# The order of 64 attention jobs: from unit by unit to a wave of four units, three batches apart

## The chip, the cores and the metric

The kernel runs on one core of one Trainium2 chip. The metric is the device time of one execution in microseconds (us), the median of several runs; lower is better.

## What is computed

Sixteen batches of 256 tokens of width 256 go through four attention units and then through a routed expert layer. Cut to what matters here:

```python
x = x + tanh(g_xattn[0]) * _L0_xattn_ref(ctx_2048, _layernorm(x), L0_xattn_b, itok)   # unit 0: keys and values are the two halves of ctx
x = x + tanh(g_ffn[0])   * _L0_ffn_ref(_layernorm(x), ...)                            # unit 1: self attention + top-2 of 8 dense experts (256 to 256)
x = x + tanh(g_xattn[1]) * _L1_xattn_ref(_layernorm(x), ctx_2048, ...)                # unit 2: self attention over own keys and ctx keys, projection
x = x + tanh(g_ffn[1])   * _L1_ffn_ref(_layernorm(x), ...)                            # unit 3: causal attention, projection, then the routed experts
```

All four attentions have 16 heads of 16 columns. Unit u of a batch needs unit u-1 of the same batch and nothing of another batch.

## The kernel before

`attention_phase` does 64 jobs `(u, b)`, four units by 16 batches, and `expert_phase` does the rest of unit 3 (routing, experts, combination); only the first is touched by the change. A job is a chain of steps. `LOADX` brings x; `LNS`, `LNP`, `LNX` normalise it on VectorE and GpSimd; `XT` turns it on TensorE. `K`, `Q`, `V` project (two turns each on TensorE, read from one of two banks `pre_ps` by ScalarE); in unit 0 `KT` and `XT` stand for K and Q, and `VC` copies the values out of the loaded context on GpSimd. `KSPLIT` and `QSPLIT` split keys and queries into three bf16 parts on GpSimd; `STACKK`, `STACKQ` store these parts to HBM and `ROWSK`, `ROWSQ`, `ROWSC` bring them back stacked by rows (`ks`, `qs`), all issued by SyncE. `S` computes the scores of a head (TensorE into `s_ps`, two banks) and VectorE takes their maximum; `M` and `MT` put the maxima of eight heads into `qs`. `T` computes the scores again, turned (TensorE into `t_ps`, two banks), and ScalarE takes their exponential; `PV` multiplies with the values, `OT` turns and divides. Unit 1 has `GATE`, `GEXP`, six `TOP` steps, `CT`, `MBIAS` and eight `EXPERT` steps; units 2 and 3 have `OTT` and `PROJ`; `FIN` adds to x and `STOREX` stores it. Unit 2 has two sources of keys, so 32 `S` and 32 `T` for 16 heads.

What sets the order: `orders()` plays the steps once, ahead of the build, with the costs in `STAGES`, takes each engine's next step by the soonest start (and by the lower job where two are close), lets no job begin that is `AHEAD_JOBS = 6` or more ahead of the first unfinished one, and writes one fixed list for each engine (`ORDER`). On the chip each engine goes through its own list in that order and waits on semaphores. Which buffer of a ring a job has follows from its place in the list `JOBS`:

```python
JOBS = [(u, b) for u in range(UNITS) for b in range(B)]
NX, NCTX, NPART, NQ, NKV, NO = 5, 2, 2, 3, 4, 3
```

So all 16 jobs of unit 0 come first, then all of unit 1, and so on. Values of the context: unit 0 lays them out in `va` and stores them (`STOREV`, 512 KB a batch, to `vc_d`); unit 2 loads them back (`LOADV`). Rows 96 to 98 of `ks` hold a bias in unit 0 alone; `UNBIAS` clears them on VectorE when the first four jobs of unit 1 take these buffers.

Of the kernel before, what the change touches and what calls it, by code (L numbers as in the profile page):

```python
# [28 lines left out]
G = 2  # L29
# [17 lines left out]

UNITS = 4
JOBS = [(u, b) for u in range(UNITS) for b in range(B)]
# [10 lines left out]

def kv_at(u, b, src=0):

    return (b, B + b, 2 * B + 2 * b + src, 4 * B + b)[u]
# [4 lines left out]
    "LOADX": [("sp", 0.4), ("wire", 4.0)], "LOADC": [("sp", 0.5), ("wire", 9.0)], "LOADV": [("sp", 0.5), ("wire", 6.5)],  # L68
    "VC": [("pool", 0.65)], "STOREV": [("sp", 0.5), ("wire", 8.5)],
# [6 lines left out]
    "UNBIAS": [("dve", 1.8)], "BPROJ": [("pool", 1.27)],  # L76
# [36 lines left out]
def job_steps(u, b):  # L113
# [15 lines left out]
    def kv_before(src):  # L129

        at = kv_at(u, b, src) - NKV
        return next(((v, c, s) for v, c in JOBS for s in range(sources(v)) if kv_at(v, c, s) == at), None)

# [27 lines left out]
    turned = add("XT", 0, s, *free)  # L161
    if u == 0:
        k = add("KT", 0, c, past("STACKK", NPART))
        q = turned
        needs[turned].append(past("STACKQ", NPART)) if past("STACKQ", NPART) else None
    else:
        k = add("K", 0, turned, past("STACKK", NPART))
        q = add("Q", 0, turned, past("STACKQ", NPART))
        values.append(add("V", 0, turned, *values_free(srcs - 1), ("STOREV", 0, kv_at(u, b) - NKV, 0) if u == 1 and b < NKV else None))
    k = add("STACKK", 0, add("KSPLIT", 0, k))  # L170
# [7 lines left out]
    clear = add("UNBIAS", 0, *keys_free(0, 0), *keys_free(0, 1)) if u == 1 and b < NKV else None  # L178
    if u == 1:
        chain = add("GEXP", 0, add("GATE", 0, turned))  # L180
        for n in range(TOPS):
            chain = add("TOP", n, chain)
        chain = add("MBIAS", 0, add("CT", 0, chain))
        experts = [add("EXPERT", (t, e), chain) for t in range(NT) for e in range(0, E, 2)]
    outs = []
    for g in range(G):
        ss = [add("S", (h, src), *rows, *keys[g]) for h in heads_of(g) for src in range(srcs)]
        m = add("MT", g, add("M", g, *ss))
        for n in range(g * HG // QH, (g + 1) * HG // QH):
            parts = [add("T", (h, src), m, clear) for h in range(n * QH, (n + 1) * QH) for src in range(srcs)]  # L190
            outs.append(add("OT", n, add("PV", n, *values, *parts)))
    if u < 2:
        add("FIN", 0, *outs, *(experts if u == 1 else []))
    else:
        add("PROJ", 0, add("OTT", 0, *outs), bp if u == 2 else None)
# [136 lines left out]
UNBIAS_AT = counted(of_kind("dve", "UNBIAS"))  # L332
# [10 lines left out]
def uses_before(kind, job, src=0):  # L343

    u, b = job
    at = {"x": JOB[job], "part": JOB[job], "q": JOB[job], "o": JOB[job], "ctx": b, "kv": kv_at(u, b, src)}[kind]
# [3 lines left out]
def row_dmas(at):  # L350

    return STACK_DMAS + (1 if at < B else 0)
# [5 lines left out]


def kv_user(at):  # L360

    for u, b in JOBS:
        for src in range(sources(u)):
            if kv_at(u, b, src) == at:
                return u, b, src
# [86 lines left out]
def build(nc, x, ctx_in, itok, g_xattn, g_ffn, key_b, w0_qkv, b0_qkv, w0_gate, b0_gate, w0_exp, b0_exp,  # L452
# [3 lines left out]
    bias_d = dram("key_bias_parts", [B, 3, T], BF16)  # L456
# [3 lines left out]
    vc_d = dram("ctx_values", [B, P, NT * H * VW], F32)  # L460
# [12 lines left out]
def attention_phase(nc, a):  # L473
    x, ctx_in, tanh_g, ident = a["x"], a["ctx_in"], a["tanh_g"], a["ident"]
    bias_d, q_d, k_d, kc_d, vc_d, x_d, h_d = (a[n] for n in ("bias_d", "q_d", "k_d", "kc_d", "vc_d", "x3_d", "h_d"))
    own = ExitStack()
    with own:
# [36 lines left out]
        keyi = xs[0][0:B, 0, :].bitcast(I32); kbf = xs[0][0:B, 1, :]; kbb = xs[1][0:B, 0, :]; kbp = pq[0][0:B, 0, :, :]  # L514
# [13 lines left out]
        ctx_loaded, vc_loaded, vc_stored = sems("ctx_loaded", NCTX), sems("vc_loaded", 2), sems("vc_stored", NKV)  # L528
# [12 lines left out]
        POOL_SETUP_STEPS = 14 + 2 * NKV  # L541
# [3 lines left out]
        with nc.Block() as block:  # L545
# [28 lines left out]
            def _(pool):  # L574
                pool.memset(power[:, :], -0.5)
                pool.memset(ident[:, :], 0.0).then_inc(pool_step, 1)
                pool.memset(late[:, :], 0.0).then_inc(pool_step, 1)
                pool.memset(own_head[:, :], 0.0).then_inc(pool_step, 1)
                pool.wait_ge(pool_step, 3)
# [5 lines left out]
                pool.wait_ge(pool_step, 4)  # L585
                pool.tensor_copy(ident_b[:, :], ident[:, :]).then_inc(pool_step, 1)
                for n in range(3):
# [3 lines left out]
                    pool.wait_ge(pool_step, 8 + n)  # L591
# [4 lines left out]
                pool.wait_ge(pool_step, 14 + NKV)  # L596
# [4 lines left out]
            def _(dve):  # L601
# [3 lines left out]
                dve.wait_ge(pool_step, 6)  # L605
# [32 lines left out]
            def _(act):  # L638
                act.wait_ge(pool_step, 10)
# [30 lines left out]
        def wait_values_free(eng, u, b, src):  # L670

            at = kv_at(u, b, src) - NKV
            if at >= 0:
                v, c, _ = kv_user(at)
                eng.wait_ge(pv_ready, PV_AT[("PV", v, c, H // QH - 1)] + 1)
                if at < B:
                    eng.wait_ge(vc_stored[at % NKV], 16 * (at // NKV + 1))

        with nc.Block() as block:
            @block.sync  # L680
            def _(sp):
                def wait_keys_free(u, b, src, g):
                    at = kv_at(u, b, src) - NKV
                    if at >= 0:
                        v, c, r = kv_user(at)
# [11 lines left out]
                for step in ORDER["sp"]:  # L697
# [14 lines left out]
                    elif name == "LOADC":  # L712
                        nth, at = uses_before("ctx", (u, b))
                        if nth:
                            wait_copied(sp, ("KT", 0, b - NCTX, 0))
                            sp.wait_ge(vc_ready, VC_AT[("VC", 0, b - NCTX, 0)] + 1)
                        sp.dma_start(ctx[at][:, :, :], tiles(ctx_in[b])).then_inc(ctx_loaded[at], 16)
                    elif name == "STOREV":
                        nth, at = uses_before("kv", (u, b))
                        sp.wait_ge(vc_ready, VC_AT[("VC", u, b, 0)] + 1)  # L720
                        sp.dma_start(vc_d[b], va[at][:, :, :, :].rearrange("p t h w -> p (t h w)")).then_inc(vc_stored[at], 16)
                    elif name == "LOADV":
                        nth, at = uses_before("kv", (u, b), 0)
                        wait_values_free(sp, u, b, 0)
                        own_at = kv_at(0, b)
                        sp.wait_ge(vc_stored[own_at % NKV], 16 * (own_at // NKV + 1))
                        sp.dma_start(va[at][:, :, :, :].rearrange("p t h w -> p (t h w)"), vc_d[b]).then_inc(vc_loaded[b % 2], 16)
                    elif name == "STACKK":
                        if u and j - NKV >= B:
                            old_u, old_b = JOBS[j - NKV]  # L730
# [4 lines left out]
                        store_parts(k_d[j % NKV] if u else kc_d[b], pk[part_at], k_stored[part_at])  # L735
# [5 lines left out]
                    elif name == "ROWSK":  # L741
# [4 lines left out]
                        if u == 0:  # L746
                            sp.dma_start(ks[at][PRODUCTS:BIAS, hs, :], bias_d[b].unsqueeze(1).broadcast_to([3, HG, T])).then_inc(k_rows[k][at], 16)
                        sp.wait_ge(k_stored[part_at], 16 * DC * (nth_part + 1))
                        stack_rows(ks[at], k_d[j % NKV] if u else kc_d[b], 1, k_rows[k][at], hs)
                    elif name == "ROWSC":  # L750
                        nth, at = uses_before("kv", (u, b), 0)
                        wait_keys_free(u, b, 0, k)
                        stack_rows(ks[at], kc_d[b], 1, k_rows[k][at], slice(k * HG, (k + 1) * HG))
# [19 lines left out]
            def _(pe):  # L773
# [29 lines left out]
                for step in ORDER["pe"]:  # L803
# [31 lines left out]
                    elif name == "CT":  # L835
                        pe.wait_ge(top_done, TOP_AT[("TOP", u, b, TOPS - 1)] + 1)
                        for t in range(NT):
                            last = pe.transpose(bank[0:E, t * P:(t + 1) * P], comb[j % 2][:, t, :], ident[:, :])
                        end_pre(step, last)
                    elif name == "MBIAS":  # L840
                        wait_copied(pe, ("CT", u, b, 0))
                        for t in range(NT):
                            last = pe.matmul(bank[:, t * D:(t + 1) * D], combt[j % 2][:, t * P:(t + 1) * P], bexp[:, :], start=True, stop=True)
# [8 lines left out]
                    elif name == "PROJ":  # L852
                        wait_copied(pe, ("OTT", u, b, 0))
                        end_pre(step, project(bank, wproj if u == 2 else wo, ott[j % 2], D, (turn,)), ends)
# [30 lines left out]
                    elif name == "T":  # L885
# [7 lines left out]
                        if u == 1 and b < NKV and step == T_FIRST[(u, b, h // HG)]:  # L893
                            pe.wait_ge(bias_set, UNBIAS_AT[("UNBIAS", u, b, 0)] + 2)
# [9 lines left out]
                    elif name == "PV":  # L904
# [36 lines left out]
            def _(act):  # L941
                for step in ORDER["act"]:
# [18 lines left out]
                    elif name == "OTT":  # L961
                        end_pre(act.activation(flat(ott[j % 2]), bank[:, :], ACT.Copy))
# [93 lines left out]
            def _(dve):  # L1056
# [792 lines left out]
```

## Time and profile before

| | |
|---|---|
| median of 3 runs | 2789.86 us (2786.05 to 2789.97) |
| the profiled execution's own time | 2787.81 us |
| its span, first to last instruction | 2786.1 us |
| mean granted TensorE clock | 0.918 |
| attention phase (first FIN at 98.1, last PROJ read at 1922.3) | up to about 1924 us |

A profile shows one execution. Busy time of an engine is the time in which one of its instructions was under way; the latency of a lone matmul counts as busy too. The granted clock is a share of 2.4 GHz: 1.00 is 2.4 GHz, 0.50 is 1.2 GHz.

### The profile page before, as it was taken

Reading aid. Unit: us, or ns where it says so; the run is one execution under the profiler, and the core shown is the slowest. Engines: PE = TensorE matmul, PEld = TensorE weight load, DVE = VectorE, ACT = ScalarE, POOL = GpSimd, SP = SyncE. Lnnn points to the kernel's source line nnn. Section 1 sums busy time; section 2 is a strip of 40 time slices with the busy share of each in tenths; the row PEclk is TensorE's granted clock in tenths of the full one; section 3 lists DMA queues with packets and bytes.
Section 4 is the critical chain, followed back from the end, with each engine's and each line's share of the span. In section 5 each row is a group of like instructions: output and inputs, shape, how many; then the busy total and the mean of one; then the engine's idle time right before and its main releaser. Section 6 shows DMA issues by size and latency. Waiting matters only on the chain. (4 is left out here: it accounts for less than half of the span.)

```text
span 2786.1 us, 50106 instructions
## 1 busy us (share of the span) xinstructions
PE 2379.2 (85%) x16356; PEld 1522.5 (55%) x16357; DVE 1626.6 (58%) x4420; ACT 1375.7 (49%) x2430; POOL 906.8 (33%) x1769
## 2 busy tenths in 40 slices
PE   3888899999999999999999999985459999999920
PEld 1445555455555565666666666652456666766710
DVE  4768796676776676676766766764562222222248
ACT  3879764453443467777777777773201111111111
POOL 5455422122222232322322376662002323222221
PEclk7989999999999999999999999996559999999965
DMA  7878533152233345555455365561730011101134
GB/s 230 212 205 209 142 89 91 35 118 55 67 87 98 89 106 122 122 122 122 117 127 122 73 160 119 126 132 57 268 129 30 30 33 32 33 32 32 32 138 171
DMA packets 206180, 300.51 MB, mean 108 GB/s; under 512 B 24918, under 2 KB 144512, under 8 KB 199585
## 3 DMA queue, kind: packets, MB, share of 16 engines
q1 hardware_dynamic: 183808, 253.78, 35.9%
q10 hardware_dynamic: 15264, 26.22, 2.7%
q0 software_dynamic: 6912, 17.97, 2.1%
q8 instruction: 115, 1.88, 0.3%
q14 instruction: 81, 0.66, 0.1%
HBM read 205.57 MB, written 93.22 MB: 107 GB/s over the span
## 5 line engine op out<-in xcount | busy, mean ns | idle before, releaser
L1112 DVE TENSOR_REDUCE mx<-s_ps 128x2 f32<-128x512 f32 (+1 forms) x1024 | 657.3, 683 | 216.0 <-PE s_ps L870 141.3
L995 ACT ACTIVATE ex<-t_ps 128x512 f32<-128x512 f32 (+1 forms) x1280 | 684.2, 577 | 193.8 <-PE t_ps L901 149.3
L901 PE MATMUL t_ps<-qs,ks 123*128 123x256 bf16 x2048 | 362.0, 278 | 9.9 <-ACT ex L995 5.8
L926 PE MATMUL pv_ps<-ex,va 128*32 128x256 f32 (+1 forms) x5120 | 325.7, 381 | 2.3 <-POOL ex L1035 2.3
L989 ACT ACTIVATE qs<-tr_ps 27x2048 bf16<-27x2048 bf16 x128 | 239.2, 1869 | 144.7 <-PE tr_ps L883 142.0
L847 PE MATMUL pre_ps<-wexp,xt 128*128 128x512 f32 x512 | 265.6, 628 | 6.7 <-DVE moe L1176 2.6
L1626 PE MATMUL x_up_ps<-wup,x_rows_t 128*128 x568 | 257.8, 597 | 1.9 <-issue 1.3
L1645 PE MATMUL x_y_ps<-wdn,x_act 128*128 x1136 | 257.0, 379 | 0.9 <-ACT x_act L1672 0.9
L901 PEld LDWEIGHTS t_ps<-qs,ks 123*128 123x128 bf16 x2048 | 175.0, 99 | 142.2 <-ACT ex L995 64.7
L1692 DVE TENSOR_TENSOR x_pre<-x_up_ps,bup 128x512 f32<-128x512 f32 x142 | 98.2, 691 | 233.0 <-PE x_up_ps L1626 233.0
L1645 PEld LDWEIGHTS x_y_ps<-wdn,x_act 128*128 128x128 f32 x1136 | 210.3, 190 | 26.8 <-issue 1.2
L876 PE MATMUL s_ps<-ks,qs 99*128 99x256 bf16 (+1 forms) x1024 | 189.6, 285 | 37.9 <-DVE mx L1112 25.4
L926 PEld LDWEIGHTS pv_ps<-ex,va 128*32 128x32 f32 x5120 | 142.5, 111 | 132.4 <-issue 50.2
L1105 DVE CUSTOM_DVE_ANT_0 s_ps<-s_ps,late 128x128 f32<-128x128 f32 (+1 forms) x512 | 166.8, 390 | 63.7 <-PE s_ps L873 63.2
L870 PE MATMUL s_ps<-ks,qs 96*128 96x256 bf16 x1024 | 185.1, 275 | 21.8 <-DVE mx L1112 16.4
L1043 POOL TENSOR_SCALAR mp<-mx 128x16 bf16<-128x16 f32 x128 | 34.7, 271 | 507.6 <-DVE mx L1112 475.4
L1672 ACT ACTIVATE x_act<-x_at_ps 128x512 f32<-128x512 f32 x142 | 77.1, 594 | 245.7 <-PE x_at_ps L1636 245.7
L999 ACT ACTIVATE ot<-pv_ps 128x256 f32<-128x256 f32 x256 | 98.8, 386 | 143.9 <-PE pv_ps L926 141.6
L876 PEld LDWEIGHTS s_ps<-ks,qs 99*128 99x128 bf16 (+1 forms) x1024 | 88.5, 100 | 141.4 <-DVE mx L1112 74.7
L1667 ACT ACTIVATE x_rows_t<-x_rt_ps 128x256 f32<-128x256 f32 x72 | 27.6, 383 | 277.9 <-PE x_rt_ps L1617 277.9
L1626 PEld LDWEIGHTS x_up_ps<-wup,x_rows_t 128*128 128x128 f32 x568 | 103.2, 192 | 105.7 <-issue 105.7
L1176 DVE SCALAR_TENSOR_TENSOR moe<-pre_ps,comb,moe 128x256 f32<-128x256 f32 x256 | 123.1, 481 | 62.4 <-PE pre_ps L847 56.1
(255 smaller groups left out, 3783.2 us busy)
## 6 DMA issues: line engine op xcount, KB each, us to landing
q_parts<-pq SPq DMA_DIRECT2D x128, 192.0 KB
qs<-q_parts SPq DMA_DIRECT2D x64, 384.0 KB, 5.0
qs<-q_parts SPq DMA_DIRECT2D x192, 128.0 KB, 5.9
k_parts<-pk SPq DMA_DIRECT2D x96, 192.0 KB
ks<-k_parts SPq DMA_DIRECT2D x96, 192.0 KB
ks<-k_parts SPq DMA_DIRECT2D x288, 64.0 KB
ks<-ctx_k_parts SPq DMA_DIRECT2D x64, 192.0 KB
ks<-ctx_k_parts SPq DMA_DIRECT2D x192, 64.0 KB
```

Of the source, the lines that this page charges most:

```text
L847: end_pre(step, pe.matmul(bank[:, :], xt_now[:, turn, t * P:(t + 1) * P], wexp[:, turn, e:e + 2, :].rearrange("p e n -> p (e n)"), start=t ...
L870: last = pe.matmul(dst[:, r * T:(r + 1) * T], q(src), key(r)[0:rows, h, :], start=True, stop=True)
L876: last = pe.matmul(dst[:, t * T:(t + 1) * T], q(t), key(0)[0:rows, h, :], start=True, stop=True)
L901: last = pe.matmul(dst[:, t * T:(t + 1) * T], key[0:ROWS, h, t * P:(t + 1) * P], qs[q_at][0:ROWS, h, :], start=True, stop=True)
L926: last = pe.matmul(pv_ps[i * VW:(i + 1) * VW, q0:T], val[:, t, k * QH + i, :], e, start=r == 0 and t == 0, stop=r == srcs - 1 and t == NT - 1,
L989: act.activation(qs[q_at][PRODUCTS:ROWS, k * HG:(k + 1) * HG, :], tr_b[PRODUCTS:ROWS, 0:T].unsqueeze(1).broadcast_to([ROWS - PRODUCTS, HG, ...
L995: act.activation(ex[:, n % EXPS, 0:w], t_ps[n % 2][:, 0:w], ACT.Exp).then_inc(t_read, 1)
L1105: last = dve.tensor_tensor_reduce(out=seen, in0=seen, in1=late[:, 2 * P - w:2 * P], scale=1.0, scalar=FUTURE, op0=ALU.add, op1=ALU.max, ac ...
L1112: dve.tensor_reduce(dst, s_ps[n % S_BANKS][:, :].rearrange("p (a b) -> p a b", a=dst.shape[-1]), AX.X, ALU.max).then_inc(s_read, 1)
L1176: last = dve.scalar_tensor_tensor(out=moe[r][:, t, :], in0=bank[:, n * D:(n + 1) * D], scalar=comb[r][:, t, e + n:e + n + 1], in1=moe[r][: ...
L1626: last = pe.matmul(up_ps[h][:, :], rows_t[:, c, :], wup[:, c, bass.ds(x, 1), h * HALF:(h + 1) * HALF].rearrange("p e f -> p (e f)"), start ...
L1645: last = pe.matmul(y_ps[:, 0:D], act_t[h][:, g * P:(g + 1) * P], wdn[:, bass.ds(x, 1), f, :].rearrange("p e n -> p (e n)"), start=f == 0, ...
```

## The change

`JOBS` becomes a wave: in round n there stand the jobs (0, n), (1, n-3), (2, n-6), (3, n-9), as far as these batches exist. Rounds 0 to 2 hold unit 0 alone, rounds 9 to 15 all four units, rounds 22 to 24 unit 3 alone. Everything that had counted jobs by unit is now counted along this list (key and value buffers, contexts, the two `ott` buffers). `STOREV` and `LOADV` are gone: unit 2 loads the values' half of the context again from the input (256 KB) and `VC` copies it on GpSimd as in unit 0. `UNBIAS` is gone: where a key buffer that held a bias goes to a job without one, a small DMA from a row of zeros clears it. The planner, its costs and `AHEAD_JOBS` stay.

```diff
-JOBS = [(u, b) for u in range(UNITS) for b in range(B)]
+BEHIND = (0, 3, 6, 9)
+JOBS = [(u, n - BEHIND[u]) for n in range(B + BEHIND[-1]) for u in range(UNITS) if 0 <= n - BEHIND[u] < B]
...
+KV_USERS = [(u, b, src) for u, b in JOBS for src in range(sources(u))]
+KV_AT = {user: at for at, user in enumerate(KV_USERS)}
...
-    return (b, B + b, 2 * B + 2 * b + src, 4 * B + b)[u]
+    return KV_AT[(u, b, src)]
...
-    if u == 0:
-        c = add("LOADC", 0, past("KT", NCTX), past("VC", NCTX))
-        values.append(add("VC", 0, c, *values_free(0), ("STOREV", 0, b - NKV, 0) if b >= NKV else None))
-        add("STOREV", 0, values[0])
-    if u == 2:
-        values.append(add("LOADV", 0, *values_free(0)))
+    if u in (0, 2):
+        before = CTX_JOBS[CTX_AT[(u, b)] - NCTX] if CTX_AT[(u, b)] >= NCTX else None
+        c = add("LOADC", 0, ("VC", *before, 0) if before else None, ("KT", *before, 0) if before and before[0] == 0 else None)
+        values.append(add("VC", 0, c, *values_free(0)))
...
-    turned = add("XT", 0, s, *free)
+    turned = add("XT", 0, s, *(free if u else []))
...
+                def bring_bias(u, b, src, g):
+                    at = kv_at(u, b, src)
+                    if row_dmas(at) > STACK_DMAS:
+                        sp.dma_start(ks[at % NKV][PRODUCTS:BIAS, g * HG:(g + 1) * HG, :],
+                                     bias_d[b if biased(at) else B].unsqueeze(1).broadcast_to([3, HG, T])).then_inc(k_rows[g][at % NKV], 16)
```

What stands on TensorE where a job of unit 2 begins its scores, batch 7, before. `s_ps<-ks,qs` is S (two matmuls a step), `t_ps<-qs,ks` is T, `pv_ps` is PV, `pre_ps<-xt,w1x` is a turn of K or Q of unit 2, `tr_ps` is MT or OT. A float32 matmul stands once in these rows and twice in the trace:

```order
L870 MATMUL s_ps<-ks,qs 128x256 x4
L791 MATMUL pre_ps<-xt,w1x 128x256 x2
L901 MATMUL t_ps<-qs,ks 128x256 x2
L870 MATMUL s_ps<-ks,qs 128x256 x2
L901 MATMUL t_ps<-qs,ks 128x256 x2
L870 MATMUL s_ps<-ks,qs 128x256 x2
L791 MATMUL pre_ps<-xt,w1x 128x256 x2
L901 MATMUL t_ps<-qs,ks 128x256 x2
L926 MATMUL pv_ps<-ex,va 32x256 x16
L883 MATMUL tr_ps<-ident_b,mp 27x128 x2
L901 MATMUL t_ps<-qs,ks 128x256 x4
L870 MATMUL s_ps<-ks,qs 128x256 x8
```

And the same place after the change, with what stands ahead of it from the last turn of that job's Q on (`pre_ps<-xt,w1x`, the first row). Between the two pieces 20 rows are left out; they hold 8 T, two PV, six turns of V, K and Q, three OT, and four XT or KT. With the second row of the second piece the scores of that job begin. L803 with `w1x` is V of unit 2, L875 is S of unit 2, L796 with `xt,w` is K and Q of unit 1, L803 with `wg` is GATE, L888 is MT:

```order
L796 MATMUL pre_ps<-xt,w1x 128x256 x2
L803 MATMUL pre_ps<-w1x,xt 128x256 x2
L927 MATMUL pv_ps<-ex,va 32x256 x8
L888 MATMUL tr_ps<-ident_b,mp 27x128 x2
```

```order
L803 MATMUL pre_ps<-wg,xt 128x8 x4
L875 MATMUL s_ps<-ks,qs 128x256 x4
L796 MATMUL pre_ps<-xt,w 128x256 x2
L875 MATMUL s_ps<-ks,qs 128x256 x4
L796 MATMUL pre_ps<-xt,w 128x256 x2
L875 MATMUL s_ps<-ks,qs 128x256 x2
L796 MATMUL pre_ps<-xt,w 128x256 x2
L875 MATMUL s_ps<-ks,qs 128x256 x4
L796 MATMUL pre_ps<-xt,w 128x256 x2
L875 MATMUL s_ps<-ks,qs 128x256 x26
L888 MATMUL tr_ps<-ident_b,mp 27x128 x2
```

Before, S and T alternate with projections in between and the scores of a job begin while the T of the job ahead are under way; after, 20 S stand with only four K and Q turns among them before the first MT of that job, and no T.

The same place on VectorE after the change (`mx<-s_ps` is the maximum of one S, the rows between are TOP steps of a job of unit 1):

```order
L1149 TENSOR_TENSOR t_1_0<-t_1_0,first 128x16
L1113 TENSOR_REDUCE mx<-s_ps 128x1 x3
L1151 TENSOR_REDUCE t_2_0<-t_1_0 128x2
L1153 TENSOR_TENSOR t_1_0<-t_1_0,t_2_0 128x16
L1156 SCALAR_TENSOR_TENSOR t_0_0<-t_1_0,pr 128x16
L1113 TENSOR_REDUCE mx<-s_ps 128x1 x26
```

VectorE has nothing but these maxima there, one after the other. A run of 26 score matmuls stands so in five rounds (unit 2, batches 5 to 9), one of 34 for batch 4 and one of 40 for batch 10; before, no run is longer than 10 outside the very first job.

## Rows read from the trace of the kernel before

**Rows 1.** The page, busy tenths of TensorE and its granted clock in 40 slices

```profile
PE   3888899999999999999999999985459999999920
...
PEclk7989999999999999999999999996559999999965
```

**Rows 2.** Windows, one stretch for each unit; the first row names the columns

```profile
core 0: us, PE busy (x) PEld busy (x) DVE busy (x) ACT busy (x) POOL busy (x), PEclk, DMA share, GB/s
90.00:370.00 280.00, 245.04 (x2216) 140.76 (x2215) 217.27 (x475) 232.10 (x387) 131.69 (x264) 0.95 0.74 188
370.00:1011.00 641.00, 604.95 (x3520) 337.90 (x3519) 447.84 (x1107) 293.29 (x538) 157.44 (x303) 0.96 0.33 80
1011.00:1590.00 579.00, 550.12 (x5034) 356.82 (x5034) 396.56 (x870) 434.23 (x739) 170.79 (x330) 1.00 0.50 116
1590.00:1923.00 333.00, 299.67 (x2662) 201.89 (x2659) 210.21 (x1107) 230.19 (x428) 209.74 (x486) 0.95 0.49 116
```

**Rows 3.** Lines of FIN and of unit 3's PROJ: count, duration, first and last start

```profile
L1197 DVE SCALAR_TENSOR_TENSOR xs<-o,tanh_g,xs x32: 750/752/1526, 98.1 to 1010.8; 128x512 f32<-128x512 f32 x32
...
L1188 DVE TENSOR_TENSOR o<-pre_ps,xs x16: 690/691/693, 1607.5 to 1922.3; 128x512 f32<-128x512 f32 x16
```

**Rows 4.** Timeline of TensorE in unit 2: start us, us, engine, line, operation

```profile
1202.72 0.38 PE L870 MATMUL s_ps<-ks,qs 96*128 96x256 bf16 x2
1202.94 0.60 PE L901 MATMUL t_ps<-qs,ks 123*128 123x256 bf16 x4
...
1203.60 1.03 PE L798 MATMUL pre_ps<-w1x,xt 128*128 128x256 f32 x4
1204.46 0.60 PE L901 MATMUL t_ps<-qs,ks 123*128 123x256 bf16 x4
...
1208.52 0.39 PE L870 MATMUL s_ps<-ks,qs 96*128 96x256 bf16 x2 [0.21 <-DVE mx L1112]
1209.11 0.39 PE L870 MATMUL s_ps<-ks,qs 96*128 96x256 bf16 x2 [0.21 <-DVE mx L1112]
...
1210.25 1.93 PE L926 MATMUL pv_ps<-ex,va 128*32 128x256 f32 x32
```

**Rows 5.** Timeline of TensorE in unit 1: two turns of expert matmuls, then S

```profile
461.16 1.88 PE L847 MATMUL pre_ps<-wexp,xt 128*128 128x512 f32 x4
462.88 0.60 PE L876 MATMUL s_ps<-ks,qs 96*128 96x256 bf16 x4
```

**Rows 6.** VectorE's maxima, from the page's costliest groups

```profile
L1112 DVE TENSOR_REDUCE mx<-s_ps 128x2 f32<-128x512 f32 (+1 forms) x1024 | 657.3, 683 | 216.0 <-PE s_ps L870 141.3
```

**Rows 7.** Groups of ScalarE in unit 2: busy us, mean ns

```profile
L976 ACT ACTIVATE pq<-pre_ps 128x512 bf16<-128x512 f32 x14 | 8.4, 602 | 0.0
```

**Rows 8.** Timeline of GpSimd and of SyncE's queue in unit 1, QSPLIT to ROWSQ

```profile
435.53 1.60 POOL L1026 TENSOR_TENSOR aq<-aq,pq 128x512 f32<-128x512 f32 x1
...
438.22 1.16 POOL L1030 TENSOR_TENSOR pq<-aq,pq 128x512 bf16<-128x512 f32 x1
...
439.46 1.22 SPq L695 DMA_DIRECT2D q_parts<-pq  x2
...
445.44 1.35 SPq L691 DMA_DIRECT2D qs<-q_parts  x3
```

**Rows 9.** DMA issues: count, KB each, median us from issue to landing

```profile
qs<-q_parts SPq DMA_DIRECT2D x192, 128.0 KB, 5.9
...
ctx_values<-va SPq DMA_DIRECT2D x16, 512.0 KB, 5.9
```

**Rows 10.** Windows of 5 us around waits of TensorE, and one of unit 2

```profile
65.00:70.00 5.00, 4.53 (x19) 1.20 (x18) 4.52 (x8) 1.87 (x1) 0.66 (x4) 0.50 0.77 221
...
280.00:285.00 5.00, 2.25 (x26) 1.16 (x26) 0.62 (x3) 4.25 (x6) 3.47 (x4) 1.00 0.46 145
285.00:290.00 5.00, 3.82 (x22) 2.27 (x26) 4.72 (x11) 1.90 (x4) 1.19 (x3) 0.52 0.65 174
...
1100.00:1200.00 100.00, 95.33 (x887) 61.14 (x889) 68.63 (x135) 77.01 (x131) 27.31 (x52) 1.00 0.52 122
```

More of the change, by code:

```diff
@@ L131, in kv_before @@
         at = kv_at(u, b, src) - NKV
-        return next(((v, c, s) for v, c in JOBS for s in range(sources(v)) if kv_at(v, c, s) == at), None)
+        return KV_USERS[at] if at >= 0 else None
     def keys_free(src, g):
@@ L145, in values_free @@
         v, c, s = kv_before(src)
-        return [("PV", v, c, H // QH - 1)]
+        return [("PV", v, c, n) for n in range(H // QH)]
     srcs = sources(u)
@@ L168, in job_steps @@
         q = add("Q", 0, turned, past("STACKQ", NPART))
-        values.append(add("V", 0, turned, *values_free(srcs - 1), ("STOREV", 0, kv_at(u, b) - NKV, 0) if u == 1 and b < NKV else None))
-    k = add("STACKK", 0, add("KSPLIT", 0, k))
+        values.append(add("V", 0, turned, *values_free(srcs - 1)))
+    before = KEY_JOBS[KEY_AT[(u, b)] - NKV] if u and KEY_AT[(u, b)] >= NKV else None
+    k = add("STACKK", 0, add("KSPLIT", 0, k), *([("ROWSK", *before, g) for g in range(G)] if before else []))
     q = add("STACKQ", 0, add("QSPLIT", 0, q), past("ROWSQ", NQ))
@@ L177, in job_steps @@
         bp = add("BPROJ", 0, s)
-    clear = add("UNBIAS", 0, *keys_free(0, 0), *keys_free(0, 1)) if u == 1 and b < NKV else None
     if u == 1:
-        chain = add("GEXP", 0, add("GATE", 0, turned))
+        chain = add("GEXP", 0, add("GATE", 0, turned, ("FIN", u, b - 2, 0) if b >= 2 else None))
         for n in range(TOPS):
@@ L194, in job_steps @@
     else:
-        add("PROJ", 0, add("OTT", 0, *outs), bp if u == 2 else None)
+        before = OTT_JOBS[OTT_AT[(u, b)] - 2] if OTT_AT[(u, b)] >= 2 else None
+        add("PROJ", 0, add("OTT", 0, *outs, last_of(*before) if before else None), bp if u == 2 else None)
     add("STOREX", 0, last_of(u, b))
@@ L345, in uses_before, with biased @@
     u, b = job
-    at = {"x": JOB[job], "part": JOB[job], "q": JOB[job], "o": JOB[job], "ctx": b, "kv": kv_at(u, b, src)}[kind]
+    at = {"x": JOB[job], "part": JOB[job], "q": JOB[job], "o": JOB[job], "ctx": CTX_AT.get(job), "kv": kv_at(u, b, src)}[kind]
     return divmod(at, {"x": NX, "part": NPART, "q": NQ, "o": NO, "ctx": NCTX, "kv": NKV}[kind])
 def row_dmas(at):
-    return STACK_DMAS + (1 if at < B else 0)
+    return STACK_DMAS + (1 if biased(at) or at >= NKV and biased(at - NKV) else 0)
+def biased(at):
+    return KV_USERS[at][0] == 0
 def k_rows_after(at):
     return 16 * sum(row_dmas(n) for n in range(at % NKV, at + 1, NKV))
[L360 to L365, printed above, removed]
 def wait_stored(eng, stored, job):
@@ L673, in wait_values_free @@
             if at >= 0:
[L674 to L677, printed above, removed]
+                v, c, _ = KV_USERS[at]
+                eng.wait_ge(pv_ready, max(PV_AT[("PV", v, c, n)] for n in range(H // QH)) + 1)
         with nc.Block() as block:
@@ L842, in _ @@
                         for t in range(NT):
-                            last = pe.matmul(bank[:, t * D:(t + 1) * D], combt[j % 2][:, t * P:(t + 1) * P], bexp[:, :], start=True, stop=True)
+                            last = pe.matmul(bank[:, t * D:(t + 1) * D], combt[b % 2][:, t * P:(t + 1) * P], bexp[:, :], start=True, stop=True)
                         end_pre(step, last)
@@ L853, in _ @@
                         wait_copied(pe, ("OTT", u, b, 0))
[L854 removed]
+                        end_pre(step, project(bank, wproj if u == 2 else wo, ott[OTT_AT[(u, b)] % 2], D, (turn,)), ends)
                     elif name == "S":
```

109 lines of the change are left out of this document (49 added, 60 removed).

## Prediction, made before the changed kernel ran

> **What bounds the kernel now.** I read the page first [rows 1]. TensorE shows nines from slice 8 to slice 27, so the attention phase looks TensorE-bound, and a new order of the jobs could then give back only some 5%. The windows by unit [rows 2] say the same at first sight: TensorE is busy 88%, 94%, 95% and 90% of units 0 to 3, VectorE 78%, 70%, 68% and 63%, ScalarE 83%, 46%, 75% and 69%. The DMA share is 0.74 in unit 0 and 0.33 to 0.50 elsewhere. Job periods follow from them and from the first and last FIN and PROJ [rows 2, 3]: unit 0 (370-98)/15 = 18.1 us, unit 1 641/16 = 40.1, unit 2 579/16 = 36.2, unit 3 333/16 = 20.8; one batch through all units costs 115.2 us.
>
> The timeline shows that "busy" flatters [rows 4]. Full-rate spacing is start to start: an S is followed by a T after 0.22 us (0.38 is its latency), a V turn by the next after 0.86, two turns of PV take 1.93, so about 0.95 each. Where TensorE waits for VectorE the starts of S are 0.59 apart, and the row still counts 0.39 of each as busy. An expert turn is 0.86 us (four matmuls in 1.72, start to start) [rows 5]. With these I count what TensorE needs for a job at full rate; the small steps (XT, OT, MT and the like) I take at 2 us a job, 4 in unit 1, an estimate by the 0.22 us of two matmuls:
> - unit 0: 16 S and 16 T x 0.22 = 7.0, four PV 3.8, small 2: 13
> - unit 1: 7.0, PV 3.8, six turns of K, Q, V 5.2, 16 expert turns 13.8, small 4: 34
> - unit 2: 32 S and 32 T 14.1, eight PV turns 7.6, eight turns of K, Q, V, PROJ 6.9, small 2: 31
> - unit 3 (causal, three quarters of the columns): S and T 5.4, PV 3.2, eight turns 6.9, small 2: 17.5
>
> Together 95.5 of 115.2 us. In the steadiest unit, 2, the full-rate share is 31/36.2 = 0.86. That is the yardstick: the rest is short waits between S and VectorE's maximum, 0.683 us each [rows 6], and between T and ScalarE. The wave cannot make a matmul shorter; it can only change this share, and it can add longer waits.
>
> **The change part by part.** *Unit 0 under cover of others.* Three unit 0 jobs still run alone at the start. The other 13 now stand between TensorE-heavy jobs, at a DMA share near the mean instead of 0.74. At the yardstick a job needs 13/0.86 = 15.1 instead of 18.1 us: 13 x 3.0 = -39.
>
> *Unit 1.* At the yardstick 34/0.86 = 39.5 against 40.1: -10 for 16 jobs. In it the granted clock is 0.96 [rows 2]: 8% of 641 us, 51 us, at 1.2 GHz, so at most 26 us lost. Part of that is already in the 10; I take -15 for both together. *Unit 3:* 17.5/0.86 = 20.3 against 20.8, 13 jobs: -6.
>
> *Better mixing.* Expert turns and projections of one unit fill the waits of another's S and T. If the share of mixed stretches rises from 0.86 to 0.89, some 1430 us of full-rate work (16 x 95.5 less the jobs still alone) take 1430 x (1/0.86 - 1/0.89) = 56 us less. Bounds: nothing (0) and 0.92 (-108). Unit 2 before already mixes projections into S and T and still sits at 0.86, so I take half: -28.
>
> *The run of scores in each round.* The order after the change shows the new cost. At the start of a unit 2 job stand 20 S with four turns of unit 1's K and Q among them, then MT, and no T. VectorE needs 20 x 0.683 = 13.7 us there and about 1.8 for the TOP steps between (some ten small instructions), 15.5; TensorE has 20 x 0.22 + 4 x 0.86 = 7.8. It waits 7.7 us, and S goes at VectorE's pace as in [rows 4]. Seven rounds (batches 4 to 10) have it: +54. In batches 0 to 3 shorter runs; I take half: 4 x 4 = +16. Below nothing it cannot be, since two score banks let TensorE be only two S ahead.
>
> *The rows of that job come late.* Its last Q turn stands only some 14 us of full-rate TensorE work ahead of its first S: counted from the order, 8 T (1.8), 3 PV (2.9), seven turns of V, K, Q (6.0), GATE (about 0.9), four XT or KT, three OT and an MT (2.5), together 14.1; with short waits 14.4. The chain it must cover: ScalarE's two copies, 0.60 each [rows 7], 1.2; QSPLIT from 435.53 to 439.38, at least 3.1 when undisturbed; STACKQ issued at 439.46 and the last ROWSQ issued near 446.3 and landed 5.9 later [rows 8, 9], 452.2, so 12.8 behind QSPLIT's end (another job of unit 1 takes 12.5). Sum 16.8, so +2.4 in seven rounds: +17. Bounds 0 (if TensorE is slowed in the cover, the wait disappears in it) and 5 (QSPLIT queued behind the M and KSPLIT of other jobs).
>
> *The clock in such a run.* At 65 to 70 us, in the first S run of the program at VectorE's pace, TensorE was 4.53 of 5 us busy and the clock stayed at 0.50; after 280 to 285, TensorE 2.25 busy, it was at 0.52 for the next 5 us [rows 10]. A half-rate clock costs nothing while VectorE sets the pace but doubles the turns among the S and the first T behind. I take 2 us a round, +14; bounds 0 and 7 a round. (The Trainium skill, "TensorE: Matmul & The Clock Gate", section on HAM oscillation, says that a loop with a wait in each iteration has the clock fall again in each iteration; by that rule, which the rows at 280 to 290 bear out for one wait, every round would pay.)
>
> *What costs nothing.* STOREV and LOADV go, 16 x 512 KB each, 5.9 us to landing [rows 9]: they were prefetches behind other jobs. 16 half contexts are loaded instead, and 16 VC of about 0.6 us lie on GpSimd, 24 to 63% busy [rows 2]. UNBIAS leaves VectorE, four times. The bias DMAs are issued on SyncE ahead of rows that wait longer. If that cover failed, 32 clearing issues of 0.45 us each (1.35 for three) [rows 8] would be 14 us.
>
> Sum: -39 -15 -6 -28 +54 +16 +17 +14 = +13. Against the profiled execution's own time, 2787.81 (2.1 below the median of the three), this gives 2801; against the median, and that is my number, 2803.
>
> **The rivals.** *B, the mix fills the waits.* If the share reaches 0.91 in the mixed stretches, mixing gives 1430 x (1/0.86 - 1/0.91) = 91 instead of 28: 2803 - 63 = 2740, faster. Break-even with before is at a share of 0.881. For it: expert turns need no ScalarE and one VectorE step of a microsecond for four matmuls, so they are ideal filler; unit 0's DMA load is spread. Against: the order puts those turns beside the T of unit 2 and 3 and leaves none for the S run.
>
> *C, the runs cost more.* The clock stays at 0.50 through the T and PV behind each run: 7 instead of 2 us a round, and the rows come 5 late: +35 and +18, 2856.
>
> *D, no late rows and no clock loss:* 2803 - 17 - 14 = 2772, or, with less from mixing, a result within 0.2% of before. It wants the chain of 16.8 to be under 14. The rows say no: 12.8 of it is one DMA chain as measured. (The Trainium skill, "DMA: Bandwidth & Descriptors", section on the anatomy of one DMA, has a DMA of 2.0 us plus its bytes at 436 GB/s; an estimate by it is 2.9 for STACKQ's 384 KB and 3.8 for ROWSQ's 768 KB, a chain of 11 and no wait. The trace disagrees for this layout: 5.9 us for one part of ROWSQ.)
>
> **How the numbers follow.** The measurement tells 0.2%, 5.6 us, from no change. Forecast A, slower, 0.45; C 0.08; B 0.33; D 0.14, two thirds of it near no change or just faster. That gives slower 0.53, same 0.11, faster 0.36. Range: from 2745 (just above B) to 2850 (just below C); A's own range is 2793 to 2835.
>
> **What would show it.** In the profile after: rounds of 115 to 120 us between the stores of unit 3 in the middle of the phase; in each, a stretch of some 15 us at the start of unit 2's scores with VectorE above 9 tenths, TensorE's starts of S 0.6 to 0.7 apart and ScalarE nearly idle, and a clock of 0.5 in it or behind it; TensorE's waits for VectorE's maxima grown, and gathered in these stretches; short waits of S of unit 2 on the rows' DMA. Unit 1's dips of the clock gone. The prediction is wrong if TensorE's waits on maxima don't grow, or if the T and expert stretches run at a share of 0.90 or more.

## The result, and the profile after

The changed kernel takes 2800.56 us (median of 6 runs, 2797.37 to 2804.15), the kernel before 2784.88 in the same session (6 runs, 2778.91 to 2789.97). The ratio is 1.0061, 95% interval 1.0044 to 1.0077: slower by 0.6%, some 16 us. The profiled execution took 2797.57 us, its span is 2795.9 and the mean granted clock 0.908, which was 0.918. DMA traffic fell from 300.51 to 288.18 MB; what that is worth by itself was not tried.

The page after: TensorE and its clock in 40 slices, and the groups of the maxima and of unit 2's S, to be held against [rows 1, 6]:

```profile
PE   2999999999898998989989999984459999999920
...
PEclk7999999999899998989989999996559999999965
...
L1113 DVE TENSOR_REDUCE mx<-s_ps 128x2 f32<-128x512 f32 (+1 forms) x1024 | 663.8, 683 | 185.7 <-PE s_ps L881 115.5
...
L875 PE MATMUL s_ps<-ks,qs 96*128 96x256 bf16 x1024 | 216.0, 311 | 39.5 <-DVE mx L1113 37.7
```

Unit 0's eights at the start have become nines, as hoped for. Unit 1's dips of the clock do not show in these slices; in a window from 98 to 700 us the granted clock rose from 0.95 to 0.99. But from the 11th slice to the 21st, where [rows 1] has a steady 9, there is now an 8 every second or third slice, in both rows, and over the phase (98 to 1925 us) the clock fell from 0.97 to 0.95. The lines of FIN and of unit 3's PROJ show where that leaves the phase:

```profile
L1193 DVE SCALAR_TENSOR_TENSOR xs<-o,tanh_g,xs x32: 751/752/1530, 91.4 to 1634.4; 128x512 f32<-128x512 f32 x32
...
L1184 DVE TENSOR_TENSOR o<-pre_ps,xs x16: 656/692/693, 685.0 to 1930.8; 128x512 f32<-128x512 f32 x16
```

The last PROJ read starts at 1930.8, where [rows 3] has 1922.3: of the 9.8 us between the two profiled spans, 8.5 lie in the attention phase. Now one round, that of batch 7 of unit 2. This is TensorE's timeline from the last Q turn of that job to its first T:

```profile
1064.33 1.03 PE L796 MATMUL pre_ps<-xt,w1x 128*128 128x256 f32 x4
...
1069.71 0.41 PE L938 MATMUL tr_ps<-ident,ot 128*128 128x128 f32 x2 [1.79 <-ACT qs L990]
...
1081.17 0.66 PE L791 MATMUL pre_ps<-ident,xn 128*128 128x128 f32 x4 [0.52 <-ACT pk L967]
1082.73 1.03 PE L803 MATMUL pre_ps<-wg,xt 128*128 128x8 f32 x8 [0.91 <-ACT xt L961]
1083.62 0.60 PE L875 MATMUL s_ps<-ks,qs 96*128 96x256 bf16 x4
1084.05 1.03 PE L796 MATMUL pre_ps<-xt,w 128*128 128x256 f32 x4
...
1087.26 1.91 PE L796 MATMUL pre_ps<-xt,w 128*128 128x256 f32 x4
1088.97 0.58 PE L875 MATMUL s_ps<-ks,qs 96*128 96x256 bf16 x2
...
1092.72 0.39 PE L875 MATMUL s_ps<-ks,qs 96*128 96x256 bf16 x2 [0.30 <-DVE mx L1113]
1093.32 0.39 PE L875 MATMUL s_ps<-ks,qs 96*128 96x256 bf16 x2 [0.20 <-DVE mx L1113]
...
1096.31 1.20 PE L875 MATMUL s_ps<-ks,qs 96*128 96x256 bf16 x4 [0.21 <-DVE mx L1113]
1097.70 1.20 PE L875 MATMUL s_ps<-ks,qs 96*128 96x256 bf16 x4 [0.19 <-DVE mx L1113]
...
1099.63 0.39 PE L888 MATMUL tr_ps<-ident_b,mp 128*27 128x128 bf16 x2
...
1101.99 0.61 PE L904 MATMUL t_ps<-qs,ks 123*128 123x256 bf16 x2
1102.39 0.64 PE L875 MATMUL s_ps<-ks,qs 96*128 96x256 bf16 x2
1102.82 0.63 PE L904 MATMUL t_ps<-qs,ks 123*128 123x256 bf16 x2
```

Three pieces can be read. **The cover**, 1065.2 (end of the last Q turn) to 1083.6: 18.4 us for 14.1 us of full-rate work, with three waits for ScalarE. **The run**, 1083.6 to the first T: 18.4 us for 8.6 (23 S x 0.22, four turns x 0.86, the MT). S goes every 0.60 us, later every 0.70 (two in 1.39). Between MT and T lie 2.36 us. **Behind it** a T and an S take 0.83 together (1101.99 to 1102.82), the next pairs 0.85, where 0.60 is usual at full clock; the granted clock is 0.50 there (last window below). The other runs are alike: in batches 4 to 10 they last 16.6 to 19.6 us from first S to first T. VectorE and ScalarE, same stretch:

```profile
1090.69 9.74 DVE L1113 TENSOR_REDUCE mx<-s_ps 128x1 f32<-128x512 f32 x15
```

```profile
1092.49 0.84 ACT L975 ACTIVATE pq<-pre_ps,bqk 128x256 bf16<-128x256 f32 x2
1100.06 1.87 ACT L990 ACTIVATE qs<-tr_ps 27x2048 bf16<-27x2048 bf16 x1 [6.74 <-PE tr_ps L888]
```

VectorE takes fifteen maxima one after the other; ScalarE idles for 6.74 us. Its copy of 1.87 us is what T waits for. Windows of the same kernel (columns as in [rows 2]):

```profile
1065.00:1083.60 18.60, 15.38 (x126) 11.02 (x125) 5.65 (x15) 14.83 (x27) 13.39 (x20) 1.00 0.62 145
...
700.00:1500.00 800.00, 737.45 (x5626) 440.21 (x5623) 545.38 (x1511) 500.46 (x879) 305.08 (x607) 0.93 0.44 109
1085.00:1090.00 5.00, 3.81 (x14) 2.54 (x14) 4.11 (x10) 0.78 (x3) 3.48 (x4) 0.66 0.71 204
1090.00:1095.00 5.00, 3.90 (x22) 1.84 (x21) 4.93 (x12) 2.36 (x7) 3.99 (x4) 1.00 0.91 224
1095.00:1100.00 5.00, 4.09 (x17) 1.05 (x18) 4.68 (x9) 0.00 (x0) 2.93 (x8) 0.62 0.91 209
1100.00:1105.00 5.00, 4.72 (x22) 2.50 (x22) 4.03 (x7) 3.66 (x4) 0.00 (x0) 0.50 0.64 187
```

The scores of unit 2 begin at 845.1, 964.0, 1083.6 and 1203.1: rounds of 118.9, 119.6 and 119.5 us, where one batch took 115.2 before. Of such a round (95.5 us of full-rate work by the prediction's count) 72.8 lie outside the cover and the run and take 82.8: a share of 0.88. The waits of TensorE from 98 to 1925 us (total, times, longest):

```profile
PE s_ps L875 <- DVE mx L1113: 37.7, 110, 4.0
PE s_ps L877 <- DVE mx L1106: 17.5, 41, 1.2
PE tr_ps L938 <- ACT qs L990: 8.8, 6, 1.8
PE s_ps L877 <- DMA qs<-q_parts: 7.9, 1, 7.9
PE s_ps L881 <- DVE mx L1113: 6.5, 15, 0.8
```

The same view before, for the same three kinds of S (L876 is S of units 0 and 1, L870 of unit 2, L872 of unit 3; after, these are L881, L875 and L877):

```profile
PE s_ps L876 <- DVE mx L1112: 22.1, 39, 3.5
PE s_ps L870 <- DVE mx L1112: 16.4, 42, 2.9
PE s_ps L872 <- DVE mx L1105: 12.3, 36, 0.8
```

Unit 2's waits on maxima grew from 16.4 to 37.7, those of units 0 and 1 fell from 22.1 to 6.5. The one visible wait on a rows' DMA, 7.9 us, is in unit 3's last job and ends at 1899.8; it is not in a run. The kernel before has no such wait (0.2 us in all); this one is nearly as long as the 8.5 us by which the phase grew.

### The profile page after: what moved, and what is told of

The parts are those of the page before. It is cut to its first block and busy times, and to the rows that moved or that the text cites. A ratio compares the mean times of both kernels' runs of the same rounds, so it can differ in the third digit from the quotient of the medians.

```text
span 2795.9 us, 50106 instructions
## 1 busy us (share of the span) xinstructions
PE 2390.9 (86%) x16356; PEld 1522.4 (54%) x16357; DVE 1643.0 (59%) x4416; ACT 1374.9 (49%) x2430; POOL 926.7 (33%) x1786
## 2 busy tenths in 40 slices
DMA packets 206450, 288.18 MB, mean 103 GB/s; under 512 B 24706, under 2 KB 148877, under 8 KB 199854
## 5 line engine op out<-in xcount | busy, mean ns | idle before, releaser
L904 PEld LDWEIGHTS t_ps<-qs,ks 123*128 123x128 bf16 x2048 | 182.0, 100 | 166.9 <-issue 60.9
L875 PE MATMUL s_ps<-ks,qs 96*128 96x256 bf16 x1024 | 216.0, 311 | 39.5 <-DVE mx L1113 37.7
L881 PE MATMUL s_ps<-ks,qs 99*128 99x256 bf16 (+1 forms) x1024 | 185.2, 279 | 22.2 <-DMA ks<-ctx_k_parts 11.4
L875 PEld LDWEIGHTS s_ps<-ks,qs 96*128 96x128 bf16 x1024 | 86.8, 106 | 146.3 <-DVE mx L1113 113.4
L1695 DVE TENSOR_TENSOR x_y<-x_y_ps,bdn 128x256 f32<-128x256 f32 x71 | 30.0, 423 | 218.7 <-PE x_y_ps L1641 218.7
```

The costliest lines, as they stand in the source:

```text
L875: last = pe.matmul(dst[:, r * T:(r + 1) * T], q(src), key(r)[0:rows, h, :], start=True, stop=True)
L881: last = pe.matmul(dst[:, t * T:(t + 1) * T], q(t), key(0)[0:rows, h, :], start=True, stop=True)
L904: last = pe.matmul(dst[:, t * T:(t + 1) * T], key[0:ROWS, h, t * P:(t + 1) * P], qs[q_at][0:ROWS, h, :], start=True, stop=True)
```

## The experiments

Theory A: the runs of scores eat what the wave gives. A "lone run" below means a stretch of TensorE's order from a unit 2 job's first S to its first MT with at least 16 S and no T; the changed kernel has nine (batches 0 and 4 to 11), the kernel before none. Experiments of different sessions are compared by their ratios to the kernel before, whose medians were 2784.88, 2782.83, 2781.21 and 2781.54; 1% is 27.8 us.

**1. The changed code in the old order.**

```diff
-BEHIND = (0, 3, 6, 9)
+BEHIND = (0, 16, 32, 48)
```

> The changed kernel with its offsets set so that the four units follow one another as before: only the side changes stay (values of the context from the input, 16 more copies on GpSimd, no stored values, no clearing on VectorE, job count rules). Theory A (the order of the jobs makes the whole difference, the side changes cost nothing): a ratio to before of 0.998 to 1.002, and one lone run of scores, at the start. Rival S (the side changes are the cost): 1.006 or more, as much as the whole change. Rival G (the side changes save DMA time and hide part of the wave's cost): 0.997 or less.

Measured: 2787.64 us, ratio 1.0017 (1.0004 to 1.0031). The side changes (context copies, bias DMAs) cost about 5 us, between 1 and 9; the order costs the other 0.44%, 12 us. Neither the order of this run nor that of the kernel before has a lone run.

**2. K and Q of unit 2 first.** The planner takes them ahead of other steps as soon as they are ready, so the chain to the rows starts earlier and S begins while T of other jobs are still in the list. Two lone runs are left (batches 3 and 7). Work and side code are those of the changed kernel.

```diff
-            pick = min((x for x in found if x[0] <= soon + NEAR_US), key=lambda x: (x[1], rank(x[2]), x[0]))
+            pick = min((x for x in found if x[0] <= soon + NEAR_US), key=lambda x: (not hasty(x[2][0]), x[1], rank(x[2]), x[0]))
...
+def hasty(step):
+    return step[0] in ("K", "Q") and step[1] == 2
```

> The changed kernel with one rule more in the planner: where steps are about equally soon, the K and Q turns of unit 2 go first, ahead of the expert turns of unit 1. It moves no other cost. Theory A (the run of scores at VectorE's pace and the thin cover of the rows cost some 8 and 2 us in each of seven rounds, and the clock 2): most of it goes, 50 to 90 us less than the changed kernel, a ratio to before of 0.975 to 0.99; TensorE's waits on the maxima of unit 2 fall from 37.7 us to under 20. Rival B (the wave is slow for another reason, as DMA or mixing): the same time as the changed kernel within 10 us, ratio 1.003 to 1.009.

Measured: 2724.67 us, ratio 0.9795 (0.9775 to 0.9815), 2.66% or 74 us less than the changed kernel. Unit 2's waits on maxima fell to 24.6 us, where under 20 was expected. The window of the middle shows the rest:

```profile
700.00:1500.00 800.00, 767.15 (x6141) 480.46 (x6139) 586.56 (x1683) 541.46 (x955) 322.42 (x649) 0.98 0.49 117
```

TensorE does 6141 matmuls in these 800 us where the changed kernel does 5626, at 0.98 instead of 0.93 of full clock.

**3. The same rule in the kernel before.**

> The kernel before, units in turn, with the same rule (K and Q turns of unit 2 go first). Theory A (the rule helps only because it mends the wave's own run of scores): no gain here, ratio 1.00 to 1.02, since the projections then stand in clumps in a unit that had them spread. Rival R (the rule is good in any order): ratio below 0.995.

Measured: 2807.39 us, ratio 1.0087 (1.0068 to 1.0106). In the old order early K and Q are no gain, they cost 24 us; they pay where they break up runs.

**4. More work in the runs.** Each S in a lone run is issued twice into the same bank (179 scores).

```diff
-                            for r in range(2):
-                                last = pe.matmul(dst[:, r * T:(r + 1) * T], q(src), key(r)[0:rows, h, :], start=True, stop=True)
+                            for _ in range(2 if step in LONE else 1):
+                                for r in range(2):
+                                    last = pe.matmul(dst[:, r * T:(r + 1) * T], q(src), key(r)[0:rows, h, :], start=True, stop=True)
```

> The changed kernel, with the two score matmuls of the lone runs (about 20 scores in nine rounds, 179 in all) done twice into the same bank, so that TensorE works where it waited; the result is the same. Clock theory (the clock falls in each run and costs some 2 us a round behind it): the clock stays near 1.00 in and behind the runs and the time is 5 to 20 us less than the changed kernel. If the clock in the run costs nothing: the same time within 4 us, since 0.44 us a score still fits under VectorE's 0.68. If TensorE does not have that room: 179 x 0.22 = up to 39 us more.

Measured: 2812.88 us, ratio 1.0106 (1.0089 to 1.0123), 12 us more than the changed kernel. The 5 to 20 us less of the clock theory are a miss, and so is "the same time within 4 us"; the result lies in the third case, in which TensorE lacks the room. The windows of the round of batch 7 show why:

```profile
1090.00:1095.00 5.00, 4.65 (x32) 3.44 (x31) 4.25 (x10) 2.76 (x8) 3.45 (x4) 1.00 0.82 218
1095.00:1100.00 5.00, 4.44 (x30) 2.36 (x31) 4.57 (x8) 0.38 (x2) 3.29 (x4) 1.00 1.03 184
1100.00:1105.00 5.00, 3.78 (x26) 1.69 (x25) 4.79 (x8) 1.87 (x1) 1.13 (x5) 1.00 0.84 227
1105.00:1110.00 5.00, 4.83 (x29) 3.12 (x27) 3.66 (x7) 3.78 (x7) 0.00 (x0) 0.66 0.71 209
```

```profile
1085.91 1.03 PE L888 MATMUL s_ps<-ks,qs 96*128 96x256 bf16 x8
...
1104.77 0.46 PE L917 MATMUL t_ps<-qs,ks 123*128 123x256 bf16 x2 [0.40 <-ACT qs L1003]
...
1432.12 16.19 PE L888 MATMUL s_ps<-ks,qs 96*128 96x256 bf16 x72 [3.51 <-DVE mx L1126]
```

The clock now stayed at 1.00 through the run, and the run took 18.9 us instead of 18.4: a doubled S at full clock goes every 0.70 us, as a single one at half clock does, so what the full clock gave back the doubled work took. What the half clock costs inside a run is therefore not shown by this experiment. By the rows of the changed kernel it is something: S every 0.70 instead of 0.60, and the K or Q turn at 1087.26 took 1.71 us to the next start instead of 0.86; an estimate from these is 1 to 1.5 us in this run. Behind the run the clock fell all the same, so the cost there was not saved. At half clock, in batch 10, 18 doubled S took 16.1 us, 0.90 each, where the single S there go every 0.70. Most of the added time came there: from the first S of batch 10 to that of batch 12 it is 9.2 us longer than in the changed kernel, of 16.2 between the two profiled spans.

**5 and 6. Half of each maximum.** The maximum of unit 2 reads 256 of its 512 columns; the other half is left out. Once in the changed kernel, once in the kernel before.

```diff
-dve.tensor_reduce(dst, s_ps[n % S_BANKS][:, :]...
+dve.tensor_reduce(dst, s_ps[n % S_BANKS][:, 0:T if u == 2 else 2 * T]...
```

> The changed kernel, with the maximum in unit 2 taken over half of the columns (256 of 512), so VectorE's part of such a score should fall from 0.683 to about 0.42 us; it leaves that half of the maximum out and nothing else. Theory A (VectorE's pace sets the lone runs): the runs of 20 scores fall from 16 to about 12 us, so 3 to 5 us in each of seven to nine rounds, 30 to 50 us less than the changed kernel in all. Rival B (TensorE or the rows' DMA sets them): under 10 us less.

> The kernel before with the same half maximum in unit 2. There scores of unit 2 lie among the T, so VectorE is 68% busy and seldom waited for. Theory A: 5 to 15 us less than before, a ratio of 0.995 to 0.998; so the changed kernel gains at least 20 us more by the same cut. If before gains as much as the changed kernel does, the run is not what VectorE costs.

Measured: in the changed kernel 2789.28 us, ratio 1.0028 (1.0016 to 1.0039), 9 us less than without it; in the kernel before 2773.17, ratio 0.9969 (0.9959 to 0.998), also 9 us less. The first is a miss, and so is the lead of 20 us over the second. The run of batch 7 in the changed kernel with half maxima:

```profile
1083.12 0.60 PE L875 MATMUL s_ps<-ks,qs 96*128 96x256 bf16 x4
...
1093.61 0.72 PE L875 MATMUL s_ps<-ks,qs 96*128 96x256 bf16 x4 [0.19 <-DVE mx L1113]
1094.52 0.72 PE L875 MATMUL s_ps<-ks,qs 96*128 96x256 bf16 x4 [0.19 <-DVE mx L1113]
...
1097.51 0.39 PE L888 MATMUL tr_ps<-ident_b,mp 128*27 128x128 bf16 x2 [0.56 <-POOL mp L1051]
...
1099.87 0.61 PE L904 MATMUL t_ps<-qs,ks 123*128 123x256 bf16 x2 [0.29 <-ACT qs L990]
```

Two S take 0.91 instead of 1.19 or 1.39, but the run lasts 16.75 instead of 18.4 us. Twenty maxima of 0.42 instead of 0.683 would be 5.3 us less. All nine runs together, first S to first T, are 18 us shorter, 2 each, and the kernel gained half of that. What is left in a run is the turns of K and Q, the TOP steps, M on GpSimd, MT, ScalarE's copy and T. The theory that a run costs VectorE's duration is too narrow. That it costs because TensorE's list holds little else there fits all these runs, but it is argued: no experiment put work of another kind into a run.

**7. Another distance.** `BEHIND = (0, 3, 7, 11)` and nothing else; three lone runs are left (batches 5, 7, 11).

> The changed kernel with the units 0, 3, 7 and 11 batches behind instead of 0, 3, 6 and 9, the planner as it is. Its order has three lone runs of scores (29 scores) where the changed kernel has nine (125). Theory A: a gain over the changed kernel in step with the runs, 30 to 70 us, ratio to before 0.98 to 0.995. Rival B (a wave itself is what costs): no gain.

Measured: 2751.94 us, ratio 0.9896 (0.9877 to 0.9914), 1.65% or 46 us less than the changed kernel. (The 29 and 125 scores of the expectation are 58 and 179 by the definition above.)

**8. K, Q and V of unit 2 first, `BEHIND = (0, 3, 6, 10)`;** no lone run is left.

> The wave with units 0, 3, 6 and 10 batches behind and with K, Q and V turns of unit 2 first. Theory A: no worse than the run with K and Q first, 2700 to 2725 us, ratio 0.970 to 0.979; waits on maxima of unit 2 under 25 us.

Measured: 2713.85 us, ratio 0.9758 (0.9739 to 0.9777), 67 us less than the kernel before: the fastest of all. Unit 2's waits on maxima are 27.3 us, where under 25 was expected.

**9 and 10. The dose.** The rule of experiment 2 for some batches only, `step[0] in ("K", "Q") and step[1] == 2 and 4 <= step[2] <= 6`, and the same with `0 <= step[2] <= 3`. Six lone runs are left in the one; in the other batch 0 loses its run, batch 3 gets one, and nine are left.

> The same rule as in the run with K and Q of unit 2 first, but for batches 4 to 6 alone. In the fixed order of TensorE this takes away three of the nine runs of scores (batches 4, 5, 6) and leaves those of batches 0 and 7 to 11. Theory R (each run costs its time, one at a time): the run with the rule for all batches took away seven runs net and 76 us, 10.8 a run; three runs give 25 to 40 us less than the changed kernel, about 2768, 0.991 to 0.996 of the kernel before. Rival M (the early K and Q help by mixing everywhere, not by the runs; or the gain comes only when the whole order has changed): less than 15 us, or more than 50.

> The same rule for batches 0 to 3 alone. In the order of TensorE no run of batches 4 to 11 goes; batch 0 loses its run and batch 3 gets one, so there are still nine. Theory R: no gain, -8 to +8 us against the changed kernel, 1.003 to 1.009 of the kernel before. Rival M (early K and Q help wherever they stand): four batches of sixteen give a quarter of the 76 us, 19 us less.

Measured: batches 4 to 6: 2764.82 us, ratio 0.9944 (0.9927 to 0.9962), 1.17% or 33 us less than the changed kernel. Batches 0 to 3: 2802.84, ratio 1.0085 (1.0065 to 1.0105), no gain. Both as expected. The starts of the S of batches 9 and 11 with the rule for 4 to 6:

```profile
1288.68 0.60 PE L879 MATMUL s_ps<-ks,qs 96*128 96x256 bf16 x4
...
1504.69 1.06 PE L879 MATMUL s_ps<-ks,qs 96*128 96x256 bf16 x4
```

and in the changed kernel:

```profile
1324.62 0.60 PE L875 MATMUL s_ps<-ks,qs 96*128 96x256 bf16 x4
...
1540.56 1.06 PE L875 MATMUL s_ps<-ks,qs 96*128 96x256 bf16 x4
```

35.9 us ahead at both: the whole gain was made before batch 9, and the rounds that kept their runs take as long as before. The starts of unit 3's PROJ reads show the same: of the first four rounds between them three take 102.4, 101.9 and 111.8 us, where the changed kernel has 118.8, 119.7 and 119.5; the next two are 118.4 and 119.4 against 120.1 and 119.5. Yet TensorE's waits for VectorE hardly show it:

```profile
PE s_ps L879 <- DVE mx L1117: 36.8, 88, 3.9
```

36.8 against 37.7. The idle time put down to maxima was not the price of a run.

**11. K, Q and V first, with (0, 3, 7, 11);** two lone runs are left (3 and 10).

> K, Q and V of unit 2 first in all batches, with units 2 and 3 a batch further behind (0, 3, 7, 11); two runs of scores are left (batches 3 and 10), where the version with (0, 3, 6, 10) has none. Theory R: within 25 us of that version, 10 to 25 us slower for the two runs, 2724 to 2739, 0.979 to 0.984 of the kernel before. Rival: the distance of the units counts by itself (less of each end of the phase is mixed, two more rounds): slower than 2745.

Measured: 2729.66 us, ratio 0.9817 (0.9796 to 0.9837), 16 us more than with (0, 3, 6, 10), within what was expected.

Lone runs removed against time saved, from the changed kernel on: with the distances kept, 3 runs and 33 us, 7 runs and 74 us, so 11 and 10.6 us a run; with other distances as well, 6 and 46, 7 and 68, 9 and 84, so 8 to 10 us a run. What the distances cost or give by themselves was not separated. Something else went along with the runs: the wait for the rows of unit 3's last job, 7.9 us in the changed kernel, stands in experiments 4, 5, 9 and 10 too (8.2 to 9.6) and is gone in 2, 7, 8 and 11. If these 8 us are taken off, experiment 2 gives 9.4 us a run and 7, 8 and 11 give 6 to 9; experiment 9 keeps its 11. So the three runs of experiment 9 cost 11 us each, and all nine 8 to 9 in the mean.

## Why the prediction came out as it did

The forecast was 2803 us; it came out at 2800.56, and the sum of +13 us stands against +16 by the medians (+10 by the two profiled executions). Step by step:

- **Rounds** of 115 to 120 us: 118.9 to 119.6.
- **Unit 0 under cover, unit 1's clock, mixing.** The share outside the runs is 0.88 in the round of batch 7; the prediction had 0.86 to 0.89 with half taken, 0.875. Rival B wanted 0.91, which this round does not reach. With the runs broken up other kernels reach 2714 to 2752, on both sides of B's 2740.
- **The run**, 15.5 us from first S to MT: 16.0. The size was right, the reason too narrow. It was worked out as VectorE's time; experiments 5 and 6 show that VectorE's rate is a small part. The prediction also ended the run at MT and left out the 2.36 us to the first T. And it charged seven runs, batches 4 to 10, where the order has nine: batch 11 has one too, and so has batch 0, which the forecast put among the shorter ones.
- **The rows come late**, 2.4 us a round. The loss in the cover is that size (18.4 against 14.1/0.88 = 16.0), but the wait named for it is not there: TensorE had lost the time on ScalarE first, the case that the prediction gave as its lower bound. That the sizes agree is luck. The forecast's sum was not consistent either: 14.1 us of work at its own share of 0.86 are a cover of 16.4, not 14.4, and leave 0.4 to wait; and its 16.8 takes 12.5 for the DMA chain where its rows give 12.8. The chain itself was about as late as forecast. Its last part in the changed kernel, from the timeline and from the page:

```profile
1075.98 1.35 SPq L697 DMA_DIRECT2D qs<-q_parts  x3
```

```profile
qs<-q_parts SPq DMA_DIRECT2D x192, 128.0 KB, 5.7
```

  The last issue near 1077 and 5.7 behind it give 1082.7, 17.5 us after the last Q turn (forecast: 16.8) and 0.9 ahead of the first S. Without ScalarE's waits (3.2 us in the three rows of the cover) S would have waited for these rows, by an estimate from these numbers. The figures that the prediction sets beside this chain are given by the Trainium skill ("DMA: Bandwidth & Descriptors", section on the anatomy of one DMA) for DMAs issued by GpSimd, and SyncE issued these, so the 5.7 us here neither confirm nor refute them.
- **The clock**, 2 us a round: behind the run about five pairs of S and T take 0.85 instead of 0.60, 1.3 us; inside it 1 to 1.5 us by the estimate above. So 2 was about right. In the changed kernel the granted clock is 0.63 to 0.81 in the runs of batches 4 to 11 and 0.97 in that of batch 0, with 0.50 in the 5 us behind; the Trainium skill's rule ("TensorE: Matmul & The Clock Gate", section on HAM oscillation), that it falls again in each such loop, agrees with that. It does not hold for every lone run: in that of batch 7 of experiment 7 (1123.3 to 1144.1) and in the 5 us behind it the clock was 1.00, with TensorE busy almost throughout.
- **The side changes at nothing:** +5 us (1 to 9). Which of them costs it was not tried.
- **The end of the phase**, not in the sum: the wait of 7.9 us for the rows of unit 3's last job.
- **Batches 0 to 3**, +16: not shown by any run; the control of experiment 10 moves nothing there.

In one round the pieces are 2.4 in the cover, 18.4 - 8.6/0.88 = 8.6 in the run, 1.3 behind it: 12.3 us; removing runs gave 8 to 11 each. Nine of them are 76 us by experiment 8 without the wait at the end and 99 by the price of experiment 9. The forecast had 101 for its four terms (54, 16, 17 and 14). The order as a whole costs 12, and 8 of it are that wait, so the rest of the wave gives some 70 to 95, where the forecast had 88. So the account of two large sums that nearly cancel was right; that they came within 3 us of the measured difference is luck, since seven runs instead of nine, the side changes and the end of the phase are off by more than that. That removing the runs gives the time is shown by experiments 2, 3, 9 and 10, of which 9 is the cleanest; its split over the three pieces is read off one round and was not tested piece by piece.

## What to carry to other kernels

A fixed order of jobs is only as good as its longest stretch in which the busiest engine has one kind of work: look in the order itself, before any run, for long runs of the step that another engine answers one by one, and ask which late input put them there. Here, with that input's chain started earlier, the same interleaving turned from 0.6% slower to 2.1% faster. The list of waits does not price such a stretch, since lone matmuls count as busy; compare its length with its work at full rate.

## What was not expected of the hardware

With two score banks, S went every 0.60 us at full clock and 0.70 at half clock, although VectorE's maximum shows 0.683; fifteen of them took 9.74 us, 0.65 each. With half maxima (0.42) S went every 0.455. Doubling the matmuls of an S at full clock also gave 0.70. These paces fit a loop through both engines better than the longer of the two alone; no run took the loop apart.

The clock fell behind a run even where TensorE had been granted 1.00 throughout it (experiment 4, 0.66 in 1105 to 1110).
